# A decoder layer on one core: the sums of each rounding round moved into the next step, limit passes placed later

## What is computed

```
x = _layernorm(x + attn(x, wq, wk, wv, wo))
x = _layernorm(x + xattn(x, ctx_512, Wq, Wkv_expand, Wout))      # causal, first 512 context rows matter
w1, w2, w3 = (nf4_dequantize(*nf4_quantize(w), w.shape) for w in (weight1, weight2, weight3))
x = _layernorm(x + (silu(x @ w1.T) * (x @ w2.T)) @ w3.T)
```

## Time and profile before

| | |
|---|---|
| runs | 1112.7, 1114.49, 1114.27 us; median 1114.27 |
| span of the profiled execution, first to last instruction | 1115.2 us |
| TensorE busy | 1029.7 us (92%) |
| VectorE busy | 754.1 us (68%) |
| ScalarE busy | 481.9 us (43%) |
| POOL busy | 431.2 us (39%) |
| granted TensorE clock, mean | 0.983 |

### The profile page before, as it was taken

How to read it: one execution, slowest core, us unless ns; L and a number is a source line. 1 busy time by engine, 2 the same in 40 slices (tenths; PEclk the granted TensorE clock), 3 DMA queues, 4 the chain that set the end, 5 groups by cost and what they waited for, 6 DMA issues and landing times.

```text
span 1115.2 us, 17521 instructions
## 1 busy us (share of the span) xinstructions
PE 1029.7 (92%) x6280; PEld 665.8 (60%) x6280; DVE 754.1 (68%) x1560; ACT 481.9 (43%) x587; POOL 431.2 (39%) x462
## 2 busy tenths in 40 slices
PE   8899899998999888989888988998999999999995
PEld 7545455554555444556455555655647888888884
DVE  7678759667865778558866876896675646464535
ACT  3343444654465455545754665575352212112110
POOL 3448675976697545123242323222256100000000
PEclk9899999999999989999999999999999999999998
DMA  6731576386636763647675575747546303011021
GB/s 233 219 84 29 128 217 186 96 236 192 194 86 168 200 170 106 164 90 176 166 168 132 120 185 140 174 118 184 128 90 211 106 1 107 7 38 39 1 76 39
DMA packets 92618, 145.16 MB, mean 130 GB/s; under 512 B 22507, under 2 KB 39795, under 8 KB 92275
## 3 DMA queue, kind: packets, MB, share of 16 engines
q1 hardware_dynamic: 83218, 116.49, 40.1%
q0 software_dynamic: 8000, 26.75, 8.6%
q10 hardware_dynamic: 1312, 0.79, 0.2%
HBM read 78.09 MB, written 23.73 MB: 91 GB/s over the span
## 4 chain that ended last, share of the span: by engine, by line
PE 68%; DVE 17%; issue 4%; DMA 4%; ACT 4%; SPq 2%; ACTq 0%; POOL 0%; DVEq 0%; POOLq 0%
PE att_pv L1045 12%; PE att_scores L982 8%; PE att_pv L1298 7%; PE att_scores L1298 7%; PE att_scores_T L1328 7%; PE att_scores_T L1018 6%; PE att_scores_T L966 6%; PE att_scores_T L968 5%; PE att_scores_T L967 5%; DVE att_mx L1661 4%; PE att_scores_T L1163 2%; DVE att_scores L1656 2%; DVE att_nf_zone L1816 2%; DMA att_probs<-nf_x 1%; ACT att_probs L1465 1%
## 5 line engine op out<-in xcount | busy, mean ns | idle before, releaser
L1465 ACT ACTIVATE att_probs<-att_scores_T 128x1024 f32<-128x1024 f32 (+2 forms) x256 | 217.6, 884 | 156.7 <-PE att_scores_T L1018 154.2
L1045 PE MATMUL att_pv<-att_probs,att_v 128*32 128x512 f32 (+3 forms) x1024 | 213.5, 532 | 0.6 <-POOL att_probs L843 0.4
L1045 PE MATMUL att_pv<-att_probs,att_ones 128*32 128x512 f32 (+3 forms) x1024 | 213.4, 532 | 0.0
L1661 DVE TENSOR_REDUCE att_mx<-att_scores 128x2 f32<-128x1024 f32 x124 | 151.5, 1222 | 88.1 <-PE att_scores L982 87.1
L982 PE MATMUL att_scores<-att_k_stack,att_q_stack 96*128 96x256 f32 (+1 forms) x504 | 167.0, 403 | 27.7 <-DVE att_mx L1661 21.9
L1018 PE MATMUL att_scores_T<-att_q_stack,att_k_stack 97*128 97x512 f32 (+2 forms) x512 | 141.6, 387 | 8.6 <-ACT att_v L1371 2.1
L1656 DVE CUSTOM_DVE_ANT_0 att_scores<-att_scores,att_cmask 128x128 f32<-128x128 f32 (+3 forms) x256 | 121.0, 511 | 38.3 <-PE att_scores L982 36.5
L843 POOL TENSOR_SCALAR_AFFINE_SELECT att_probs<-att_probs 128x256 f32<-128x256 f32 x128 | 57.3, 448 | 190.6 <-ACT att_probs L1465 187.8
L982 PEld LDWEIGHTS att_scores<-att_k_stack,att_q_stack 96*128 96x128 f32 x504 | 87.0, 193 | 72.2 <-DVE att_mx L1661 31.5
L1018 PEld LDWEIGHTS att_scores_T<-att_q_stack,att_k_stack 97*128 97x128 f32 x512 | 87.3, 193 | 51.8 <-issue 18.6
L1555 ACT ACTIVATE att_probs<-att_scores 128x512 f32<-128x512 f32 x44 | 26.3, 598 | 206.8 <-PE att_scores L1298 206.8
(11 more groups left out here) (262 smaller groups left out, 2095.3 us busy)
## 6 DMA issues: line engine op xcount, KB each, us to landing
att_q_stack<-att_q_hi SPq DMA_DIRECT2D x128, 128.0 KB, 3.1
att_probs<-nf_x SPq DMA_DIRECT2D x28, 352.0 KB, 3.7
att_nf_home<-nf_reciprocals POOLq DMA_DIRECT2D x48, 176.0 KB, 4.8
att_q_stack<-att_q_lo SPq DMA_DIRECT2D x64, 128.0 KB, 3.6
att_k_stack<-att_k_hi SPq DMA_DIRECT2D x64, 128.0 KB, 3.4
att_nf_home<-nf_x SPq DMA_DIRECT2D x20, 352.0 KB, 3.6
w_nf<-att_nf_zone SPq DMA_DIRECT2D x192, 22.0 KB, 2.6
att_k_stack<-att_k_hi SPq DMA_DIRECT2D x64, 64.0 KB, 3.4
```

Source lines behind the costliest of these rows:

```text
L1045: last = T.matmul(pv[HD * j:HD * j + HD, sums, q0:S], lhs, pr[:, at:at + S - q0], start=(t == 0), stop=(t == TT - 1))
L1465: A.activation(probs_of(b, r)[:, 1024 * h:1024 * h + w], bank[:, 0:w], ACT.Exp, scale=SCALE).then_inc(st_free, 1)
L1661: V.tensor_reduce(mx[:, p % 2, :].rearrange("p (r t) -> p r t", r=2)[:, :, t], sco[:, :, :], AX.X, ALU.max).then_inc(sc_free, 1)
```

## The change

The sums of a step's last round leave the end of the step and are made in the next step, behind the second half of the weighing and ahead of the transposed maxima; its scaling moves on VectorE behind the next step's first maxima. The place in the ring moves with them. Since the fetch of round u waits for the sums of round u - 1, limit passes are placed later: on ScalarE pass 0 now always follows the last exponential, and its further passes follow the copies of projections; on VectorE the passes stand behind the third maxima (but for the steps called quick), and in step 1 at the end. Rounds called `mid` keep their sums.

```diff
--- before.py
+++ after.py
@@ -119,6 +119,11 @@
     return tuple((us if len(us) == 2 else [None] + us) + [None, None])[:2]
 
 
+def late_round(b, p):
+
+    return rounds_of(*after(b, p, -1))[1]
+
+
 def pieces_of(b, p):
 
     if crossed(b):
@@ -176,6 +181,8 @@
     for b in range(NB):
         for p in range(NP):
             order += [("exp", b, p, 0), ("exp", b, p, 1)]
+            if late_round(b, p) is not None:
+                order.append(("round", late_round(b, p)))
             if after(b, p, 1):
                 order.append(("rows", *after(b, p, 1)))
             if crossed(b) and p == 0:
@@ -192,8 +199,6 @@
                 order += [("sums",), ("rec",)]
             if (b, p) == (1, 0):
                 order.append(("dq",))
-            if end is not None:
-                order.append(("round", end))
     return order + [("out", NB - 1, k) for k in range(2)]
 
 
@@ -1216,6 +1221,8 @@
                     if pairs(b, p) > 0:
                         weigh(*back, 2)
                         weigh(*back, 3)
+                    if late_round(b, p) is not None:
+                        rounding(late_round(b, p))
                     if turn1:
                         turn_maxima(*turn1)
                     if fore:
@@ -1256,8 +1263,6 @@
                     if not ahead:
                         weigh(b, p, 0)
                     weigh(b, p, 1)
-                    if end is not None:
-                        rounding(end)
                     if (b, p) == (0, 4):
                         bank = bank_for(("sums",))
                         pe.wait_ge(tot_ok, 1)
@@ -1509,22 +1514,13 @@
                         for what in values_of(b):
                             evacuate(b, what)
                     exponential(b, p, 2)
-                    if mid is not None:
-                        for k in scalar_passes(mid):
-                            exceed(mid, k)
-
-                    behind = crossed(b) and p in (3, 6)
-                    if mid is None and 0 in mine and not behind:
-                        exceed(end, 0)
                     exponential(b, p, 3)
-                    if mid is None and 0 in mine and behind:
-                        exceed(end, 0)
+                    for k in scalar_passes(mid) if mid is not None else mine[0:1]:
+                        exceed(end if mid is None else mid, k)
                     if (b, p) == (B - 1, 1):
                         act.wait_ge(wq_in, 32)
                         for h, src in enumerate((rsw, rsum)):
                             hi_of_weights(wh[:, 2 * h:2 * h + 2, 256:768], src)
-                    for k in mine if mid is not None else mine[1:]:
-                        exceed(end, k)
                     if halved(b, p):
                         hi_of_x(*halved(b, p))
                     if (b, p) == (B - 1, 2):
@@ -1538,6 +1534,8 @@
                             hi_of_weights(wh[:, k, 1024:1536], y[:, k, :])
                     for what in made(b + 1, p):
                         evacuate(b + 1, what)
+                    for k in mine if mid is not None else mine[1:]:
+                        exceed(end, k)
                     if (b, p) == (0, 4):
                         copy_scalers(("sums",), sumf, NW)
                         copy_scalers(("rec",), rec_t, NW * P)
@@ -1858,10 +1856,12 @@
                 for p in range(NP):
                     fore = after(b, p, LEAD)
                     G = pairs(b, p) // 2 - 1
-                    mid, end = rounds_of(b, p)
+                    (mid, end), before = rounds_of(b, p), late_round(b, p)
                     if p == 1 and b > 0:
 
                         maxima(*fore, 0)
+                        if before is not None:
+                            scale_rounded(before)
                         maxima(*fore, 1)
                         exceeds(mid, range(4))
                         add_residual(b - 1, 0)
@@ -1869,19 +1869,19 @@
                         if mid is not None:
                             scale_rounded(mid)
                         moments(b - 1, 0)
-                        exceeds(end, (1, 2, 3))
                         add_residual(b - 1, 1)
                         maxima(*fore, 3)
-                        if end is not None:
-                            scale_rounded(end)
                         moments(b - 1, 1)
                         if not late(b):
                             begin_spread(range(TT))
                         for what in made(b + 1, p):
                             cut_raw(b + 1, what)
+                        exceeds(end, (1, 2, 3))
                         continue
                     if fore:
                         maxima(*fore, 0)
+                        if before is not None:
+                            scale_rounded(before)
                         largest_behind(b, p, 0)
                     if (b, p) == (0, 0):
                         begin_half(3)
@@ -1924,8 +1924,7 @@
                         scales_of_scalers()
                         quantise_scalers()
 
-                    beside = 0 < b < B - 1 and p == 6
-                    if not beside:
+                    if quick:
                         exceeds(end, (1, 2))
                     if fore and not quick:
                         maxima(*fore, 2)
@@ -1935,7 +1934,7 @@
                         V.tensor_copy(qh[:, 2:4, :], pvr[:, :, :]).then_inc(first_hi, 1)
                     if quick:
                         maxima(*fore, 3)
-                    exceeds(end, (1, 2, 3) if beside else (3,))
+                    exceeds(end, (3,) if quick else (1, 2, 3))
                     if quick and b > B and p == 5:
                         scale_rows(range(2, TT), TT - 1)
                     if crossed(b) and b + 1 < NB and p == 3:
```

## The result

The changed kernel takes 1155.05 us (median of four runs, 1151.16 to 1164.62) against 1113.87 us: a ratio of 1.0375, 95% interval 1.0341 to 1.0409. The direction was forecast, the size was not: +41 us where +13 stood, and 1155 lies outside the range. In this document medians are over all executions of a kernel, while ratios leave out those that ran long: one of `self_only` (1137.1 us), one of `sums_step0` (1124.7) and two of `early_fetch_sums` (1617 and 5427). The profiled execution has a span of 1153.7 us, 38.5 more than before.

A forecast was written before the change was run, and what follows sets the result against it. TensorE, busy 92% of the span, was taken as the bound, so gains and losses come through its waits. Terms +15.9, +8.1, +4.9 and -15.9 gave +13.0 us, forecast 1127, range 1115 to 1141.

The forecast's parts named there:

- the nine steps: Steps with two ScalarE limits (pairs 2, 4, 5 of batches 4 to 6): late rows and copies lengthen them, +15.9 us.
- The walk of (5,4): Batch 5, step 4, followed engine by engine: interval between second score pairs grows from 9.28 to 11.15 us, +1.9.
- I keep 3.0 of it: Steps 7 and 0: maxima behind limits that wait for the fetch make TensorE wait at the next maxima, 3.0 us.
- Rival 2: Slower still: new waits in nine steps halve TensorE's clock, up to +15 us, 1142; chance 0.12, shared with stacks ahead of rows.
- Step 1: VectorE's three limits there now stand next to the following step's maxima: 1.2 us per self batch, 0.4 per cross batch.
- The other 34: Remaining moved rounds, new wait for the scaling: 16 cross-phase at 0.36 us, 18 self-phase at 0.13, +8.1 together.
- What goes: Old TensorE waits before sums (14.7 us) and before maxima's products in batch 3 (4.2) vanish, 3.0 kept: -15.9 us.
- The landing: Fetch of the next round's rows by SyncE: 3.6 us from issue to landing, the median of 48 earlier fetches.
- Rival 1: Faster: limits stay hidden and only waits go, 1108.6 us; needs step 4's rows landed at 4.9 or copies unchained; chance 0.11.

The follow-up runs named there:

- self_only: Kernel before, with sums and limits late only in batches 1 to 3 (self phase): 1130.14 us, ratio 1.0179.
- sums_step0: Kernel before, with only the rounds of step 0 of batches 2 to 7 summed late, all limits in old places: 1114.88 us, ratio 0.9998.
- early_fetch_sums: Kernel before, with sums late, limits in old places, next rows fetched once limit passes have read the last ones (weights differ): 1113.52 us, ratio 0.9988.
- maxima_first: Changed kernel, with VectorE's limits in steps 7 and 0 behind the fourth maxima instead of ahead: 1153.98 us, ratio to the kernel before 1.0357.
- cross_only: Kernel before, with sums and limits late only in the cross phase (batches 4 to 7): 1142.48 us, ratio 1.0248.
- limits_alone: Kernel before, with limits late as in the change but sums and scaling at the step's end as before: 1190.65 us, ratio 1.0691.
- fetch_scalar: Kernel before, with sums late, only ScalarE's limits moved, rows fetched once limit passes have read the last ones (weights differ): 1141.76 us, ratio 1.0242.
- set 3: Four late-sums kernels: one with early fetch, two with one engine's limits moved, one with only step 0's sums late: 1113.52 to 1164.49 us.

## Why the prediction was right or wrong

- **Direction, and the mechanism of the nine steps: right.** The walk of (5,4) held to 0.5 us at every point. Its sum, +15.9 against +15.7, is right by luck in two ways. By steps, 4 to 5 was put at 5.7 and measured 3.8, 2 to 3 at 7.2 and 5.3, 5 to 6 at 3.0 and 6.7. And the walk counted waits alone, where only 9.1 of the 15.7 is idle time and the rest is slower matmuls, with 12.6 us more at half clock. In 5 to 6 there is a misreading: "the stacks are used three steps on, so only the rows matter, except in step 6". In step 5 the next batch's first stacks stand behind the rows, stores and scales in SyncE's queue and are used one step on, in the maxima; four such waits came to 7.7 us.
- **"In steps 7 and 0 the maxima stand behind limits that wait for the fetch ...: I keep 3.0 of it": the step that failed.** The mechanism was named and its size guessed, not walked. The eight waits are 18.5 us, and the clock fell at each of the five long ones. A walk like that of (5,4) would have shown them. In step 7 before, the transposed maxima start at t = 3.6; the sums take that place, the fetch goes at 4.4, rows land at 8.0, and VectorE's three limits (1.95 us for two, 0.6 for the last) end near 10.6. Measured: 4.7, 8.2 and 11.5. TensorE is done with its other work at about 9.7, and the reduction takes 0.8 us more, so the walk, an estimate from these rows, gives a wait of 1.7 us; 2.70 to 2.74 were measured in the cross phase. At (2,1) the landing of 6.5 us, near the top of the earlier trace rows and not its median, came on top. `maxima_first` shows that it isn't the order alone: the wait moves to the sums.
- **"Rival 2, the clock": it came true beside the forecast, not instead of it.** 11 more half-clock stretches, 16.6 us more busy time; +15 stood in the rival. It was kept out of the sum, a term put at nothing, because one wait of 2.09 us before had been followed by no drop. That says that a wait of this length need not bring the clock down, not that nine or twenty will not. And "the trace's repeated waits of 1 us never did it" misreads the trace before: the half-clock stretch at 615.9 stands behind a wait of 0.90 us and no longer one, those at 441.8 and 568.0 behind 1.68 and 1.56.
- **Step 1, "1.2 us on the two self batches, 0.4 on each of four cross batches": too small.** In step 2 the sums of step 1's round wait 1.94 to 2.08 us in six of seven batches and 0.74 us in batch 3: 12.6 us of the 15.4 left before the sums.
- **"The other 34": right or a bit high.** In plain self steps the interval grows 0.13 to 0.26 at steps 4 and 5 and nothing at 6, into which no round moves; line 1023 waits for the scaling 11 times, 0.2 us at most, where 0.36 stood for 16.
- **"What goes, -15.9": the old waits before the sums did go, but 12.6 us came back in step 2.** Batch 3 did not become shorter: 1.2 us longer. One interval of it, 1 to 2, is 4.9 us shorter; the 2.77 us wait of the earlier trace rows and the low clock behind it are missing there, as they are in `cross_only`, where batch 3 has the code of the kernel before (a wait of 0.22 us stands in its place there), so this is no gain of the change, and a sign that the 2.77 us wait belongs to one execution more than to the program.
- **The landing, 3.6 us: right.** After, 3.3 to 6.5, median 3.5. The 2.8 us estimated by the Trainium skill's "DMA: Bandwidth & Descriptors" (Anatomy of one DMA) is below every one; the section gives that rule for transfers issued by GpSimd, and SyncE issues these.
- **The rivals.** Rival 1 needed rows at t = 4.9; they landed at 6.4. With early rows and old places, which is about what it asked for, the time is 1113.5 and not 1108.6: even then the waits taken away were no gain.

What stays open: what decides, from run to run, behind which waits the clock falls, and how the 28 us of late limits divide outside step 1.

## What to carry to other kernels

A consumer moved later moves its producer's refill later too, and the refill is met first where the least other work stands between the producer's output and what is queued behind it, here at the batch boundary: walk that step, not only the typical one. Where two delays use the same slack, testing one alone says little; a small table of both, each way, showed here that late sums are free once the rows come early, and that late rows and late limits are not. When a change adds waits to TensorE in a recurring place, put the matmuls behind them at half clock into the sum as a term of its own. Here it was 16.6 us beside 21.8 us of new idle time; in the other profiled executions that took over 10 us longer it ran from 0.4 of the new idle time (`limits_alone`, 23.0 to 51.3) to twice it (`fetch_scalar`, 17.0 to 8.2).

## What the runs showed of the hardware beyond this

The same program varied by 14 us (`self_only`, from 1119.1 with a granted clock of 0.985 to 1133.1 with 0.978). The new waits are not what makes a kernel unsteady: beside set 3 the kernel before spread as far in 21 executions (1107.1 at 0.989 to 1121.6 at 0.982), and `limits_alone`, with the longest waits of all, stayed within 4 us. One profile may show a kernel at its best, as that of `self_only` did, 11 us below its median.
